# Channel attention with queries and keys replicated for two batches at once, head scores moved ahead of the turned maxima, values scaled on GpSimd, and a router of transposed logits

## The reference, cut to what matters

```
x += tanh(g_xattn[0]) * gated_attention(layernorm(x), ctx)          # stage 1
x += tanh(g_ffn[0])   * mixture_of_experts(layernorm(x))            # stage 2
x += tanh(g_xattn[1]) * channel_attention(layernorm(x), ctx, ctx)   # stage 3
x += tanh(g_ffn[1])   * nvfp4_mlp(layernorm(x))                     # stage 4

# stage 2: logits = x @ router_w.T (32 experts); probs = softmax(logits);
#          the top 8 of a row, divided by their sum, weigh silu(x@wg) * (x@wu) @ wd of each expert
# stage 3: per batch q, k, v are (64, 256) seen as 8 heads of 8 rows by 256 columns
#          qk = einsum('bhdq,bhdl->bhql', qh, kh) / sqrt(8);  sm = softmax(qk)
#          ret = gamma * einsum('bhql,bhdl->bhdq', sm, vh)
```

## Time and profile before

| | |
|---|---|
| time, 3 runs | median 1010.79 us, 1010.21 to 1011.31 |
| profiled execution | 1012.7 us, of which the span of the page is 1010.9 |
| busy in the span | PE 88%, PEld 72%, DVE 73%, ACT 56%, POOL 28% |
| stage 2 (opening, then steps) | 454.6 to 698.4 |
| stage 3 | 698.8 to 848.8 |
| a batch of stage 3 in its middle | 7.58 us |

### The profile page before, as it was taken

The page is one execution under the profiler, slowest core; times in us unless marked ns, Lnnn a source line. Parts: engine busy times, 40 slices in busy tenths (PEclk is TensorE's granted clock), DMA queues, the critical chain, the costliest instruction groups (busy, mean ns, idle before and its releaser), DMA issues. The chain is left out here.

```text
span 1010.9 us, 18481 instructions
## 1 busy us (share of the span) xinstructions
PE 890.1 (88%) x6890; PEld 729.4 (72%) x6892; DVE 734.0 (73%) x1242; ACT 564.2 (56%) x1713; POOL 281.1 (28%) x417
## 2 busy tenths in 40 slices
PE   1678999999999999879899999997898886899997
PEld 1678888888888889866677777775455553677776
DVE  7878898989898988786544444446688887666653
ACT  5677878777787877724333333323466664233332
POOL 1133434343333333413322222202211112242220
PEclk9888999999999999977899999999699998999999
DMA  4101010101010100006011111001000000101001
GB/s 149 43 1 64 2 64 1 64 2 64 1 64 2 64 2 23 1 1 247 1 50 51 51 50 50 3 0 63 1 2 2 1 2 32 63 32 44 19 0 42
DMA packets 10929, 35.74 MB, mean 35 GB/s; under 512 B 1248, under 2 KB 5344, under 8 KB 8544
## 3 DMA queue, kind: packets, MB, share of 16 engines
q1 hardware_dynamic: 10704, 34.64, 9.6%
q10 hardware_dynamic: 144, 0.03, 0.0%
HBM read 33.62 MB, written 1.05 MB: 34 GB/s over the span
## 5 line engine op out<-in xcount | busy, mean ns | idle before, releaser
L236 PE MATMUL ps<-wt_hi,xq 128*128 128x256 f32 (+1 forms) x512 | 125.4, 281 | 20.5 <-DVE ctx_lo L824 14.7
L236 PE MATMUL ps<-wt_lo,xq 128*128 128x256 f32 (+1 forms) x512 | 125.1, 285 | 0.0
L236 PEld LDWEIGHTS ps<-wt_hi,xq 128*128 128x128 f32 x512 | 101.0, 197 | 23.3 <-DVE ctx_lo L824 15.1
L414 ACT ACTIVATE square<-ps 128x128 bf16<-128x128 f32 x384 | 100.9, 295 | 27.6 <-PE ps L236 27.6
L236 PEld LDWEIGHTS ps<-wt_lo,xq 128*128 128x128 f32 x512 | 100.7, 197 | 0.0
L1652 ACT ACTIVATE ca_probs<-ps 128x512 f32<-128x512 f32 x128 | 69.5, 594 | 41.1 <-PE ps L1581 41.1
L1229 POOL TENSOR_TENSOR moe_w_lo<-moe_w_all,moe_w_hi 128x384 fp32r<-128x384 f32 x48 | 52.9, 1139 | 141.1 <-ACT moe_w_hi L1332 141.1
L572 POOL TENSOR_TENSOR rstd<-rstd,half_neg 128x6 f32<-128x6 f32 x64 | 87.3, 1364 | 5.0
L1711 DVE TENSOR_REDUCE context_mx<-ps 128x4 f32<-128x1024 f32 x64 | 76.3, 1214 | 15.7 <-PE ps L1556 15.6
L414 ACT ACTIVATION_READ_ACCUMULATOR square<-ps 128x1 f32 x384 | 86.0, 227 | 0.0
L1396 DVE TENSOR_TENSOR moe_act_g<-moe_act_g,ps 128x512 f32<-128x512 f32 x48 | 33.1, 689 | 71.1 <-PE ps L1266 71.1
(11 more groups left out here) (217 smaller groups left out, 2600.5 us busy)
## 6 DMA issues: line engine op xcount, KB each, us to landing
moe_w_all<-in_experts SPq DMA_DIRECT2D x8, 1152.0 KB, 5.2
w_in<-in_wt SPq DMA_DIRECT2D x8, 1024.0 KB, 5.8
wp_in<-in_wp SPq DMA_DIRECT2D x8, 512.0 KB, 3.6
ffn_codes<-in_codes SPq DMA_DIRECT2D x8, 384.0 KB, 3.1
ffn_w_scales<-in_code_scales SPq DMA_DIRECT2D x8, 384.0 KB, 3.8
x_rows<-in_x SPq DMA_DIRECT2D x2, 512.0 KB, 4.8
ctx_in<-in_ctxT SPq DMA_DIRECT2D x1, 1024.0 KB, 9.2
context_rows<-in_ctx SPq DMA_DIRECT2D x1, 1024.0 KB, 9.6
```

What stands on the lines that cost most here:

```text
L236: last = mm(ps[:, first + bank, col:col + width], left[:, c, tokens], w[:, c, wcol:wcol + width], start=(j == 0), stop=(j == len(steps) - 1))
L414: last = nc.scalar.activation(square[:, i % 2, j, :], ps[:, bank, (j % 4) * P:(j % 4) * P + P], ACT.Square, scale=float(HD) ** -0.5, accum ...
```

## The change

**Router.** The logits are made transposed. The 32 router columns are the stationary operand, unsplit f32, and the turned rows move, 256 at a time; four quarters of the rows go to four groups of 32 partitions of one bank. That is 16 matmuls (2 depths by high and low, by 4 quarters) in place of 48. ACT copies the bank (`scalar_quarters`), and two transposes on PE bring the logits back to rows. The split of the router's weights is gone.

**Context.** ACT's and DVE's work on the context moves from the opening into steps 2, 4, 6 and 8 of the first twelve half steps. One ACT instruction is new: it scales the values (`context.turned`) by gamma and the gate (`scalar_values`), so that `scale_values` in stage 3 becomes a product of two tensors.

**Stage 3.** `replicate` handles two batches in one matmul of 512 columns, in even batches alone, each of the two matrices in a bank of its own; `qk_rows` has four slots in place of three. `column_scores` waits for each head's bank by itself. `column_scores(b, 3)` stands ahead of `turn_maxima(b + 1)` and `row_scores(b + 2, 0)`. Scaling and adding of the values goes to POOL, except for the last batch; `turn_back` stands in the odd batches, between two maxima.

```diff
 # Router.tensor_logits
-        pe.wait_ge(self.split, 2)
-        for n in range(TILES):
-            steps = [(c, l, w) for c in range(CH) for l, w in ((k.hT_hi, self.r_hi), (k.hT_hi, self.r_lo), (k.hT_lo, self.r_hi))]
-            for j, (c, left, w) in enumerate(steps):
-                last = nc.tensor.matmul(k.ps[:, 3, n * E:n * E + E], left[:, c, n * P:n * P + P], w[:, c, :],
+        pe.wait_ge(self.r_in, 16)
+        steps = [(c, left) for c in range(CH) for left in (k.hT_hi, k.hT_lo)]
+        for j, (c, left) in enumerate(steps):
+            for q in range(P // E):
+                tiles = left[:, c, :].bitcast(F32).rearrange("p (t q n) -> p q t n", t=2, q=P // E)[:, q]
+                last = nc.tensor.matmul(k.ps[q * E:q * E + E, 3, 0:HID].rearrange("p (t n) -> p t n", t=2), self.r_rows[:, c, :], tiles,
                                         start=(j == 0), stop=(j == len(steps) - 1))
+        last.then_inc(self.quarters_ready, 1)
+        pe.wait_ge(self.quarters_copied, 1)
+        for t in range(2):
+            last = nc.tensor.transpose(k.ps[:, 3, HID + t * P:HID + t * P + P], self.quarters[:, t * P:t * P + P], k.ident[:])
...
 # gated_mlp, ACT: in the first steps, after unit(n)
+                            if moe and first and n in (2, 4):
+                                k.context.scalar(act, n // 2 - 1)
+                            if moe and first and n == 6:
+                                k.context.scalar_constants(act)
+                            if moe and first and n == 8:
+                                k.context.scalar_values(act)
...
                 turn.scalar(act)
                 high(0, 0, False)
-                k.context.scalar(act)
+                router.scalar_quarters(act)
                 router.scalar_exponent(act)
-                k.context.scalar_constants(act)
...
 # gated_mlp, DVE
+                            if moe and first and n in (4, 8):
+                                k.context.vector(dve, n // 4 - 1)
...
-                k.context.vector(dve)
                 router.vector_choose(dve)
...
 # channel_attention, PE
             def replicate(b, group):
...
                 for which, src in enumerate((split, c_split)):
-                    last = mm(ps[:, B_BANK + n % 3, which * HID:which * HID + HID], spread[:, 2 * group + which, :], src[:, b, :],
-                              start=True, stop=True)
-                last.then_inc(s["b_ready"], 1)
+                    n = b_use["rows", b, group, which]
+                    if n >= 3:
+
+                        pe.wait_ge(s["b_taken"], n - 2)
+                    mm(ps[:, B_BANK + n % 3, :], spread[:, 2 * group + which, :], src[:, b:b + 2, :].rearrange("p b f -> p (b f)"),
+                       start=True, stop=True).then_inc(s["b_ready"], 1)
...
 # column_scores
-                pe.wait_ge(s["b_taken"], n - 1)
                 for e in range(2):
+
+                    pe.wait_ge(s["b_taken"], n + e - 2)
                     group, rows = cut(2 * pair + e)
...
                 column_scores(b, 2)
-                if b + 2 < BATCH:
+                if b % 2 == 0 and b + 2 < BATCH:
                     replicate(b + 2, 1)
                 weigh(b, 0)
+                column_scores(b, 3)
                 if b + 1 < BATCH:
                     turn_maxima(b + 1)
                 if b + 2 < BATCH:
                     row_scores(b + 2, 0)
-                column_scores(b, 3)
...
 # channel_attention, POOL
+            def scale_values(b):
+                pool.wait_ge(s["inverted"], b + 1)
...
+                for t in range(2):
+                    scale_rows(nc.gpsimd, b, t).then_inc(s["scaled"], 1)
+
+                    pool.wait_ge(s["scaled"], 2 * b + t + 1)
...
             for b in range(2, BATCH):
                 values(b)
+                if b > 2 and b % 2 == 0:
+                    add_values(b // 2 - 2)
+                scale_values(b - 2)
```

More of the change, by code:

```diff
@@ L944, in gpsimd, with split_high, split_low @@
                 nc.gpsimd.memset(self.vmask[:, par, :, head, col:col + 1], 1.0)
-def split_high(copy, split, rows, first, last, done):
-    for par in range(2):
+def split_high(copy, split, rows, first, last, done, pars=(0, 1)):
+    for par in pars:
         dst = split[0:64].rearrange("p (n b) f -> p n b f", b=2)[:, first:last, par]
         copy(dst, rows[64 * par:64 * par + 64, first:last]).then_inc(done, 1)
-def split_low(nc, split, rows, first, last, done):
-    for par in range(2):
+def split_low(nc, split, rows, first, last, done, pars=(0, 1)):
+    for par in pars:
         pairs = split[:].rearrange("p (n b) f -> p n b f", b=2)[:, first:last, par]
@@ L1605, in _ @@
             replicate(0, 1)
-            row_scores(0, 0)
-            replicate(1, 0)
-            row_scores(0, 1)
-            replicate(1, 1)
-            for pair in range(2, PAIRS):
+            for pair in range(PAIRS):
                 row_scores(0, pair)
-                keep_busy(nc, k, OUT_BANK, 1)
+                if pair >= 2:
+                    keep_busy(nc, k, OUT_BANK, 1)
             turn_maxima(0)
@@ L1657, in _ @@
                 split_high(nc.scalar.copy, split, h, t, t + 1, s["h_high"])
[L1658 to L1660 removed]
+            for group in range(2):
+                take_rows(0, group)
             for b in range(BATCH):
[L1662 removed]
+                if b % 2 == 0 and b + 2 < BATCH:
                     take_rows(b + 2, 0)
@@ L1765, in _ @@
                     maxima(b + 1, 1)
+                if b > 2 and b % 2 == 1:
+                    turn_back((b - 3) // 2)
+                if b + 1 < BATCH:
                     maxima(b + 1, 2)
```

146 lines of the change are left out of this document (77 added, 69 removed).

## The result

The changed kernel is slower: median 1020.19 us (20 runs, 1009.75 to 1022.97) against 1010.90 for the kernel before beside it (20 runs, 1009.91 to 1013.21); the ratio is 1.0066, 95% interval 1.0046 to 1.0087 (it is near that of the means, 1.0068; the medians stand at 1.0092). The forecast was 1005.1, with 998.5 to 1010.5 as its range: the change came out on the other side. The runs are spread over 13 us, and time goes with the mean granted clock: the fastest had 0.960 and 0.963, those at 1020 had 0.945 to 0.947, those at 1022 0.937 to 0.948. The profiled execution took 1022.51 us, near the slow end, of which the span is 1020.7.

A forecast was written before the change was run, and what follows sets the result against it. It took DVE's late-starting router chain to bound the opening, PE the expert body, and a PE-ACT loop stage 3. Terms -6.5 + 0 + 0 + 0.8 = -5.7 took the median from 1010.79 to 1005.1 us, range 998.5 to 1010.5.

The forecast's parts named there:

- Router, -6.5: Stage 2's opening: earlier router logits and chain gain 7.0 us, less 0.5 for POOL; bounds -2.4 and -9.4.
- context, 0: Context work in the expert half steps fits beside PE's work: cost 0, up to +2 us.
- the 0.5 charged for POOL's side: Stage 2's opening: POOL's subtractions beside DVE's chain were expected to lose 0.5 us, the amount DVE lost.
- Odd batches, 7.03 by DVE's loop: Stage 3's batches without replicas: DVE's loop sets 7.03 us per batch, -0.5.
- Even batches, 8.05: Stage 3's batches making both replicas: 8.05 us per batch, +0.5, with PE waiting for ACT's copy.
- What PE saves in replicas it gives back where column scores 3 used to run beside row scores: Stage 3: the reason given for calling the whole rewriting of the loop a wash, 0 us.
- Rival 5: Stage 3: replicas hold two of three banks, slowing even batches while odd keep 7.58; 1021.9, or 1013.5 with half; chance 0.08.
- Values on GpSimd: Stage 3: POOL's copies 1.2 us, two products about 1.2, half an addition 0.4, covered by a batch of 7.
- Or this would be the larger loop everywhere: Stage 3: without scaling on POOL, which takes 0.7 us out of DVE's loop, that loop would be the larger everywhere.
- Start and end, +0.8: Stage 3's ends: first row scores +0.54, batch 0's column scores at the lower clock +1.0, final unpacking -0.7.
- stands under DVE's 3.5 us split in both kernels and counts nothing: Stage 3, batch 1: DVE's split covers this batch in both kernels, so it adds 0 to the batch sum.
- rival 3: Stage 2's opening: the clock stays low, router gains only 2.4 us; 1009.2 in all; chance 0.10.

The follow-up runs named there:

- stage2_only: Changed kernel with the old stage 3, keeping the new router and the context's new places; 1002.94 us against 1010.64 for the kernel before.
- old_replicas_dve: Changed kernel with each batch's replicas made by themselves and the values back on DVE; 1005.81 us against 1012.16 for the kernel before.
- filler_batch1: Changed kernel with four unread matmuls in batch 1's 3.56 us wait alone; 1005.55 us against 1010.92 for the kernel before.
- spread_split: Changed kernel with DVE's 3.5 us split of batch 1 cut into one-tile pieces, one in every second batch; 1031.73 us against 1010.79 for the kernel before.
- spread_filler: spread_split with one unread 128-row f32 matmul in each of its two new waits; 1009.60 us against 1011.46 for the kernel before.
- filler_first: Changed kernel with three more unread matmuls in stage 3's first wait alone; 1014.82 us against 1010.92 for the kernel before.
- fill_rows32: Changed kernel with 16 unread fp32r matmuls of 32 rows in batch 1's wait; 1020.62 us against 1011.46 for the kernel before.
- longer_wait: stage2_only with two unread DVE subtractions ahead of batch 1's split, lengthening PE's wait; 1008.99 us against 1010.79 for the kernel before.
- c3_late: Changed kernel with column scores 3 back behind the turned maxima and next row scores; 1009.24 us against 1010.64 for the kernel before.
- old_replicas: Changed kernel with each batch's replicas made by themselves again; 1004.69 us against 1010.64 for the kernel before.
- best_spread: Changed kernel with single-batch replicas, unread matmuls in the first and batch 0's waits, and DVE's split in one-tile pieces; 1021.42 us against 1010.79 before.

## Why the prediction was wrong, step by step

- **Router, -6.5 and context, 0**: right, a little small. The pick came 5.39 us earlier (5.2 expected). From the pick to stage 3's first replicas it is 218.16 us where it was 219.99, 1.83 less: the 1.8 of the clock is there, and the 0.5 charged for POOL's side is not (POOL's six pieces took 5.99 against 5.77; PE's first expert matmul waited for this 0.22, and it is in the 5.39). That is 7.2 in the profile and 7.7 in stage2_only's median. DVE's chain took 8.09 us beside POOL's pieces where it took 8.15 before, and its product at 469.04 took 0.43: nothing is seen of the waits of 0.96 by which the prediction let it end at 477.0. The context's work in the steps left no new PE wait (198.48 us busy of 199.80 from 490.2 to 690).
- **Odd batches, 7.03 by DVE's loop**: 6.89, and by that loop: DVE does not wait from 785.10 to 790.97, and PE waits 0.33 for its transpose.
- **Even batches, 8.05**: 8.49; the mechanism was right (two of three banks with replicas, PE waiting 0.45 for ACT), the size 0.4 short. From this comes the 1.7 us over seven pairs where I had 0.
- **"What PE saves in replicas it gives back where column scores 3 used to run beside row scores"**: this reason is wrong though the sum was near. The early column scores 3 gain 0.38 a batch with single replicas, the own waits 0.1, and the replicas for two batches at once lose 0.6 a batch (15.38 against 14.18 a pair). Rival 5 had this mechanism, and it got 0.08 as a whole; at the full clock the loss is far below the 7.7 from which it decides.
- **Values on GpSimd**: covered, as said. A product took 0.40 there against 0.348 on DVE, with one operation less in it, and 0.29 on DVE for the same instruction (old_replicas_dve). The factor of two that the Trainium skill gives in GPSIMD Engine Reference, section 3.1, would have made it 0.70, an estimate from the 0.348; the measurement decides. Where the two engines do meet, DVE pays: in the changed kernel the two products of the last batch, on DVE beside POOL's subtractions for stage 4, took 1.76 us (854.00 to 855.76). "Or this would be the larger loop everywhere" did not hold with single replicas: 7.10 a batch with the values on DVE.
- **Start and end, +0.8, and of batch 1 "stands under DVE's 3.5 us split in both kernels and counts nothing"**: this is the step that failed. The split ends when it did, but PE comes to its wait 1.7 us earlier and idles 3.56 us. I counted PE's idle time there as free because another engine set the end. It costs the clock of the 55 us behind it: 14.6 us (1020.19 against 1005.55 for filler_batch1; 13.0 by the ratios). With only the opening at the lower clock, which is what I had assumed, the kernel takes 1005.55, beside a forecast of 1005.1. I charged 1.0 us for the clock in batch 0 and gave no rival in which it falls later on; rival 3 had it in stage 2 only, though a lower clock beyond 480 stood among the signs of being wrong. The nearness of 1005.55 to 1005.1 is partly luck: the router gave 7.2 in place of 6.5, and the loop took 1.7 in place of 0.

Two rules of the Trainium skill speak to this, both in TensorE: Matmul & The Clock Gate. Section "A second HAM failure mode: psum-queue depth-cycling" tells of another kernel in which frequent short idle times between groups of matmuls let the clock go to and fro between its two levels; spread_split's trace agrees (0.88 and 1.28 us, four low stretches). The stretch at 784 in spread_filler has no such idle times ahead of it. The table in "Part 1: The HAM clock gate" has the full clock come back once PE stays busy; here PE was busy for 21.98 of 23.00 us and the clock stayed at 0.50; the measurement decides.

**What stays open.** Why a low stretch lasts 4 us behind one wait and 23 behind another of the same loop; why the clock fell once more at 760, behind waits of 0.45 us that the later batches have too without a fall (in spread_filler it fell at 784 in the same way; the one at 760 was there in the two profiles whose opening is that of the changed kernel in every row, and in none of the other six with replicas for two batches and the split in one piece, filler_first and fill_rows32 among them); and why the old order holds the clock better than the new one at nearly the same wait (longer_wait against the changed kernel); and what begins and keeps the long stretches of c3_late and old_replicas, where batch 1's wait was short. The small share of the array that the score matmuls use is a candidate that fits fill_rows32, but how dense each order is was not varied by itself. The 3 to 3.7 us by which the old stage 3's start and first batches are faster with fillers were not taken apart either.

## What to carry to other kernels

When a change lets TensorE arrive earlier at a wait that another engine sets, its idle time grows, and in a loop of small matmuls that can cost the clock of many us behind it (here 15 us): price the wait by the clock that follows, not only by its end. Try a few unread matmuls that use all 128 rows in the longest waits before judging a reordering (here 16 to 18 us, and the sign of the result). Undo the parts one at a time even when the sum looks flat: over fourteen batches, an estimate from the batch lengths at the full clock, early column scores gain 5 us with single replicas (0.38 a batch), and the replicas for two batches lose 8 (1.20 a pair).

## What the runs showed of the hardware

- Once TensorE's granted clock had fallen to 0.50 in this loop, it stayed there for 23.9 us in the changed kernel, 41 in c3_late, 48 in old_replicas_dve and 82 in best_spread (786 to 868), though PE was busy nearly without a gap (21.98 of 23.00 us in the changed kernel, 45.25 of 47.80 in old_replicas_dve, 59.73 of the 61.30 up to the last turned maxima in best_spread).
- Sixteen fp32r matmuls of 32 rows in a wait did not keep the clock from falling, sixteen of 128 rows did, with PE busy throughout in both profiles (3.40 of 3.40 us and 3.90 of 3.90; medians 1020.6 and 1006.4 us).
- The clock also fell behind 10 us in which PE was busy for 9.30 with no wait over 0.44 us (spread_filler, 774 to 784).
- The same kernel's time varied over 13 us with the clock's course (1009.75 to 1022.97), and over 24 in spread_split, where the kernel before stays within 6.
